# Attention and gated FFN layer on one core: mask copies on VectorE, the first group's maxima as rows without DRAM, one transpose per group, raw weights spread over four batches

## The reference, cut to what matters

```python
# x: (8, 512, 256); 16 heads of 16; Wq, Wk, Wv: (16, 256, 16); FFN 256 -> 768 -> 256
q, k, v = (einsum('btc,hcd->bhtd', x, W) + b  for (W, b) in (q, k, v))
scores  = einsum('bhtd,bhsd->bhts', q, k) * 0.25
probs   = softmax(scores + causal)                    # over s <= t
y       = einsum('bhts,bhsd->bhtd', probs, v).reshape(8, 512, 256)
x = layernorm(x + y @ Wo + bo)
wq8(w)  = w.astype(float8_e4m3fn).astype(float32)      # the FFN weights are rounded to FP8
fuse = silu((x @ wq8(gate_w)) * gate_s) * ((x @ wq8(up_w)) * up_s)
x = layernorm(x + (fuse @ wq8(down_w)) * down_s)
```

## Time and profile before

| | |
|---|---|
| median of 3 runs | 587.77 us (587.28 to 589.21) |
| the profiled execution, its own time | 586.83 us |
| its span | 585.1 us, 1.73 us less than its time |
| PE (matmul) busy | 541.7 us, 93% |
| PE weight loads | 358.9 us, 61% |
| VectorE (DVE) | 457.4 us, 78% |
| ScalarE (ACT) | 324.9 us, 56% |
| GpSimd (POOL) | 232.0 us, 40% |
| mean granted TensorE clock | 0.971 |
| DMA | 68.22 MB, mean 117 GB/s |

### The profile page before, as it was taken

The page is one execution under the profiler, slowest core; times in us unless marked ns, Lnnn a source line. Parts: engine busy times, 40 slices in busy tenths (PEclk is TensorE's granted clock), DMA queues, the critical chain, the costliest instruction groups (busy, mean ns, idle before and its releaser), DMA issues.

```text
span 585.1 us, 10840 instructions
## 1 busy us (share of the span) xinstructions
PE 541.7 (93%) x4002; PEld 358.9 (61%) x4002; DVE 457.4 (78%) x805; ACT 324.9 (56%) x579; POOL 232.0 (40%) x253
## 2 busy tenths in 40 slices
PE   8358799999999999999999999988899999999992
PEld 4134346556556565665655655645468888888892
DVE  6875657788888888888878888887546898888885
ACT  3005546766767667766676676764764444355440
POOL 8204332434333443353243433331245444565442
PEclk9698979999999999999999999999899999999997
DMA  6692847456454654553745654430000011110112
GB/s 217 179 269 84 256 112 201 146 148 186 149 141 157 190 153 150 135 185 112 201 146 148 177 160 140 144 78 3 2 1 0 2 37 36 37 38 0 38 37 72
DMA packets 59615, 68.22 MB, mean 117 GB/s; under 512 B 4074, under 2 KB 53866, under 8 KB 59562
## 3 DMA queue, kind: packets, MB, share of 16 engines
q1 hardware_dynamic: 58710, 66.59, 38.7%
q10 hardware_dynamic: 852, 0.93, 0.5%
HBM read 37.63 MB, written 29.62 MB: 115 GB/s over the span
## 4 chain that ended last, share of the span: by engine, by line
PE 82%; DVE 5%; DMA 5%; issue 3%; ACT 2%; POOL 1%; SPq 0%; POOLq 0%; DVEq 0%; ACTq 0%
PE ps L1068 15%; PE ps L939 13%; PE ps L931 12%; PE ps L856 9%; PE ps L848 9%; PE ps L1077 7%; PE ps L915 7%; PE ps L916 4%; PE ps L879 2%; DVE nmax L611 2%; PE ps L872 2%; DMA m_scratch<-mrow 2%; PE ps L890 1%; DVE part L561 1%; DMA q_st<-zero_rows 1%
## 5 line engine op out<-in xcount | busy, mean ns | idle before, releaser
L611 DVE TENSOR_REDUCE nmax<-ps 128x2 f32<-128x1024 f32 (+1 forms) x192 | 196.9, 1041 | 74.2 <-PE ps L916 73.9
L447 ACT ACTIVATE probs<-ps 128x512 f32<-128x512 f32 x320 | 183.4, 594 | 83.9 <-PE ps L931 83.7
L370 POOL TENSOR_SCALAR_AFFINE_SELECT probs<-probs 128x512 f32<-128x512 f32 x128 | 86.5, 689 | 204.6 <-ACT probs L447 204.6
L931 PE MATMUL ps<-q_st,k_st 98*128 98x384 bf16 (+3 forms) x512 | 123.3, 304 | 9.0 <-DMA q_st<-m_scratch 5.3
L915 PE MATMUL ps<-k_st,q_st 98*128 98x256 bf16 (+2 forms) x384 | 83.2, 277 | 15.6 <-DMA k_st<-k_scratch 9.3
L398 POOL TENSOR_TENSOR f_l<-f_full,f_h 128x512 fp32r<-128x512 f32 x48 | 63.4, 1323 | 73.0 <-ACT f_h L532 73.0
L916 PE MATMUL ps<-k_st,q_st 124*128 124x128 bf16 x512 | 85.0, 222 | 0.0
L939 PE MATMUL ps<-probs,v_st 128*32 128x512 f32 (+3 forms) x1024 | 84.8, 450 | 0.2
L931 PEld LDWEIGHTS ps<-q_st,k_st 98*128 98x128 bf16 x512 | 44.2, 98 | 54.7 <-issue 27.4
L527 ACT ACTIVATE sgate<-ps,s_gate 128x512 f32<-128x512 f32 x48 | 32.8, 685 | 60.0 <-PE ps L1068 60.0
L915 PEld LDWEIGHTS ps<-k_st,q_st 98*128 98x128 bf16 x384 | 37.8, 99 | 37.3 <-issue 18.6
(11 more groups left out here) (94 smaller groups left out, 852.2 us busy)
## 6 DMA issues: line engine op xcount, KB each, us to landing
q_st<-q_scratch SPq DMA_DIRECT2D x32, 384.0 KB
k_st<-k_scratch SPq DMA_DIRECT2D x32, 384.0 KB
q_scratch<-part SPq DMA_DIRECT2D x16, 384.0 KB, 3.6
k_scratch<-part SPq DMA_DIRECT2D x16, 384.0 KB, 2.6
xT<-in_attn_xT SPq DMA_DIRECT2D x8, 512.0 KB, 3.9
q_scratch<-part SPq DMA_DIRECT2D x16, 256.0 KB, 3.8
resid<-in_attn_x SPq DMA_DIRECT2D x8, 512.0 KB, 3.7
k_scratch<-part SPq DMA_DIRECT2D x15, 256.0 KB, 2.1
```

Source lines behind the costliest of these rows:

```text
L370: pool.affine_select(out=blocks, in_=blocks, compare_op=ALU.is_ge, fill=0.0, base=0, pattern=[*pattern, [1, P]], channel_multiplier=-1).th ...
L447: act.activation(probs[:, u, :], ps[:, u % 2, :], ACT.Exp, scale=SCALE).then_inc(exp_done, 1)
L611: dve.tensor_reduce(nmax[:, i, heads[0]:heads[-1] + 1], src, AX.X, ALU.max, negate=True).then_inc(max_taken, 1)
L931: m = pe.matmul(ps[:, u % 2, c0:c0 + T - P * j], k_st[0:RP, g, h, P * j:P * j + P], q_st[0:RP, g, h, P * j:T], start=True, stop=True)
```

## The change

- **Masks.** All four `fill_mask` copies run on VectorE: q for groups 0-1 and 2-3 at the start, k for groups 0-1 after the first two `first_lo`, k for groups 2-3 after the last two.
- **First maxima.** For w = 0, `first_rows` makes 16 transposes of 2 columns each, into PSUM banks 0 and 6, with the two parts on partitions 0 and 1; ScalarE and VectorE copy two heads each straight into q_st (2 x 1024). `scores(0, 0)` waits for these copies, and no DMA is left between them.
- **One transpose.** `transpose_max` is one transpose of all 32 columns of mpart; mrow becomes 32 partitions x 128, and `m_scratch` is laid out accordingly, so that rows of 256 B instead of 1 KB are stored, and 256 B pieces are read.
- **Order on TensorE.** `scores(0, 0)`, `scores(0, 1)` and the first half of the projection work stand among the maxima of group 1; fewer `keep_warm` there, 12 instead of 4 before the first stack.
- **DMA order.** b_o leaves the start (now with the late constants), xT of batch 1 goes behind the first two stacks, x of batch 0 and gate_w behind mrow of group 1; up_w is loaded in batch 1 and down_w in batch 3, behind the stacks of the next batch.
- **Quantizing.** No steps for w = 0 and 1; three for w = 2 to 29, six for w = 30 and 31.
- **add_bias** of batch n runs at g = 1 of batch n itself, the first too.

```diff
@@ -30,8 +30,8 @@
...
     HW = 32
-    NCONST = 3
-    NLATE = 4
+    NCONST = 2
+    NLATE = 5
@@ -42,7 +42,7 @@
...
     k_scratch = nc.dram_tensor("k_scratch", (H * D, NP, T), BF16, kind="Internal").ap()
-    m_scratch = nc.dram_tensor("m_scratch", (G, RM * HG, T), BF16, kind="Internal").ap()
+    m_scratch = nc.dram_tensor("m_scratch", (G, TB, RM, HG, P), BF16, kind="Internal").ap()
@@ -94,7 +94,7 @@
...
         mpart = carve(TB * 2 * HG, BF16).rearrange("p (b a h) -> p b a h", b=TB, a=2)
-        mrow = carve(T, BF16)
+        mrow = carve(P, BF16)
@@ -115,6 +115,8 @@
...
+        row_halves = [ps[0:RM, bank, :].bitcast(BF16) for bank in (0, YB)]
@@ -141,6 +143,7 @@
...
         mT_full, mT_out = sem("mT_full"), sem("mT_out")
+        rows_full, rows_out = sem("rows_full"), sem("rows_out")
@@ -206,7 +209,7 @@
...
                 eng.wait_ge(lo_ready[k], B)
-                eng.wait_ge(mrow_stored[k], 16 * B)
+                eng.wait_ge(mrow_stored[k], 16 * (B if k else B - 1))
@@ -241,11 +244,12 @@
...
                 sp.wait_ge(mT_out, n * G + g + 1)
-                sp.dma_start(m_scratch[g], mrow[0:RM * HG, :]).then_inc(mrow_stored[g], 16)
+                sp.dma_start(m_scratch[g].rearrange("i a h p -> (i a h) p"), mrow[0:TB * RM * HG, :]).then_inc(mrow_stored[g], 16)
...
             def load_mrow(n, g):
-                sp.wait_ge(mrow_stored[g], (n + 1) * 16)
-                sp.dma_start(q_st[0:RM, g], m_scratch[g].rearrange("(a h) t -> a h t", h=HG)).then_inc(mrow_loaded[g], 16)
+                sp.wait_ge(mrow_stored[g], (n + 1 if g else n) * 16)
+                sp.dma_start(q_st[0:RM, g].rearrange("a h (i p) -> a h i p", i=TB),
+                             m_scratch[g].rearrange("i a h p -> a h i p")).then_inc(mrow_loaded[g], 16)
@@ -267,21 +271,18 @@
...
             sp.dma_start(w_v[:], wv.rearrange("(k p) n -> p k n", p=P)).then_inc(const_in, 16)
-            for dst, src in ((b_v, bv), (b_o, bo)):
-                sp.dma_start(dst[:], src.partition_broadcast(P)).then_inc(const_in, 16)
-            load_xT(1)
+            sp.dma_start(b_v[:], bv.partition_broadcast(P)).then_inc(const_in, 16)
...
             sp.dma_start(k_scratch[0:P, 0:3, :], part[:, 1, :, :]).then_inc(part_stored[1], 16)
-            sp.wait_ge(mask_filled, 2)
+            sp.wait_ge(mask_filled, 3)
...
             load_stack(0, 1)
+            load_xT(1)
...
             store_parts(0, 3)
-            sp.wait_ge(mask_filled_late, 3)
+            sp.wait_ge(mask_filled, 4)
             load_stack(0, 2)
-            load_raw(0)
-            load_x(0)
@@ -289,22 +290,24 @@
...
                 if n == 0:
-                    load_raw(1)
                     sp.dma_start(w_o[:], wo.rearrange("(k p) n -> p k n", p=P)).then_inc(late_in, 16)
-                    sp.dma_start(s_down[:], down_s.partition_broadcast(P)).then_inc(late_in, 16)
+                    for dst, src in ((b_o, bo), (s_down, down_s)):
+                        sp.dma_start(dst[:], src.partition_broadcast(P)).then_inc(late_in, 16)
...
                         sp.dma_start(dst[:], src).then_inc(late_in, 16)
+                    load_x(0)
+                    load_raw(0)
...
                 load_mrow(n, 2)
-                if n == 0:
-                    load_raw(2)
...
                     load_stack(n + 1, 1)
+                if n in (1, 3):
+                    load_raw((n + 1) // 2)
@@ -349,14 +352,11 @@
...
             pool.memset(k_st[0:RM, 2:G].rearrange("p g h t -> p (g h t)").bitcast(F32), ONES).then_inc(mask_filled_late, 1)
-            pool.wait_ge(pool_const, CONSTS)
-            for stack, rows in ((q_st, mask_q), (k_st, mask_k)):
-                fill_mask(pool, stack, rows, 2).then_inc(mask_filled_late, 1)
...
                 if n == 0:
-                    pool.wait_ge(const_in, 16 * NCONST)
+                    pool.wait_ge(late_in, 16 * NLATE)
@@ -374,15 +374,14 @@
...
-            add_bias(0)
...
                         lo_part(n + 1, g)
-                    if g == 1 and n + 1 < B:
-                        add_bias(n + 1)
+                    if g == 1:
+                        add_bias(n)
@@ -428,9 +427,9 @@
...
                 act.wait_ge(mT_full, w + 1)
-                if w:
-                    act.wait_ge(mrow_stored[(w - 1) % G], ((w - 1) // G + 1) * 16)
-                act.activation(mrow[0:RM * HG, :], max_bf[0:RM * HG, 0:T], ACT.Copy).then_inc(mT_out, 1)
+                v = w - 1
+                wait(act, mrow_stored[v % G], (v // G + 1 if v % G else v // G) * 16)
+                act.activation(mrow[0:TB * RM * HG, :], max_bf[0:TB * RM * HG, 0:P], ACT.Copy).then_inc(mT_out, 1)
@@ -474,11 +473,9 @@
...
                 mid_part(0, m, probs[:, m, :])
-            empty_mT(0)
-            act.wait_ge(mT_out, 1)
-            act.dma_start(m_scratch[0], mrow[0:RM * HG, :]).then_inc(mrow_stored[0], 16)
-            act.wait_ge(mrow_stored[0], 16)
-            act.dma_start(q_st[0:RM, 0], m_scratch[0].rearrange("(a h) t -> a h t", h=HG)).then_inc(mrow_loaded[0], 16)
+            act.wait_ge(rows_full, 1)
+            act.activation(q_st[0:RM, 0, 0:2, :].rearrange("a h t -> a (h t)"), row_halves[0], ACT.Copy).then_inc(mT_out, 1)
@@ -549,7 +546,8 @@
...
             dve.wait_ge(pool_const, 5 + MG)
-            fill_mask(dve, q_st, mask_q, 0).then_inc(mask_filled, 1)
+            for g in (0, 2):
+                fill_mask(dve, q_st, mask_q, g).then_inc(mask_filled, 1)
@@ -596,6 +594,10 @@
...
+            def first_step(w):
+                return 3 * (w - 2) + 3 * max(w + 2 - W, 0)
@@ -675,9 +677,8 @@
...
                 first_lo(k + 1)
-                if k == 0:
-                    dve.wait_ge(pool_const, 6 + 2 * MG)
-                    fill_mask(dve, k_st, mask_k, 0).then_inc(mask_filled, 1)
+                dve.wait_ge(pool_const, 6 + 2 * MG)
+                fill_mask(dve, k_st, mask_k, k).then_inc(mask_filled, 1)
@@ -688,6 +689,9 @@
...
                     take_max(w, u)
+                    if w and u == 0:
+                        dve.wait_ge(mT_full, 1)
+                        dve.tensor_copy(q_st[0:RM, 0, 2:4, :].rearrange("a h t -> a (h t)"), row_halves[1]).then_inc(rows_out, 1)
@@ -696,7 +700,8 @@
...
                         take_max(w + 2, 0)
-                    quantize(3 * w)
+                    if w > 1:
+                        quantize(first_step(w))
@@ -719,7 +724,8 @@
...
                         normalize_y(w - 1)
-                    quantize(3 * w + 1)
+                    if w > 1:
+                        quantize(first_step(w) + 1)
@@ -730,11 +736,16 @@
...
                         empty_v(n + 1, 1)
-                    quantize(3 * w + 2)
+                    if w > 1:
+                        quantize(first_step(w) + 2)
...
                         split_max(w + 2)
+                    else:
+                        for q in range(3):
+                            quantize(first_step(w) + 3 + q)
@@ -868,9 +879,16 @@
...
                     pe.wait_ge(ynT_out, 2 * (w // G - 1) + w % G)
-                for i in range(TB):
-                    m = pe.transpose(max_bf[0:RM * HG, P * i:P * i + P], mpart[:, i].rearrange("p a h -> p (a h)"), ident_bf[:])
-                m.then_inc(mT_full, 1)
+                pe.transpose(max_bf[0:TB * RM * HG, 0:P], mpart.rearrange("p i a h -> p (i a h)"), ident_bf[:]).then_inc(mT_full, 1)
+            def first_rows():
+                pe.wait_ge(mpart_ready, 1)
+                for v in range(2):
+                    for h in range(2):
+                        for i in range(TB):
+                            m = pe.transpose(row_halves[v][:, T * h + P * i:T * h + P * i + P], mpart[:, i, :, 2 * v + h], ident_bf[:])
+                    m.then_inc(mT_full if v else rows_full, 1)
@@ -903,12 +921,13 @@
...
                     if w == 2:
-                        pe.wait_ge(mask_filled_late, 3)
+                        pe.wait_ge(mask_filled_late, 1)
+                        pe.wait_ge(mask_filled, 4)
...
                 wait(pe, max_taken, NM * w + u - 1)
-                if u == 1:
-                    wait(pe, mT_out, w)
+                if u == 1 and w > 1:
+                    pe.wait_ge(mT_out, w)
@@ -918,8 +937,11 @@
...
                 g = w % G
-                if u == 0:
-                    pe.wait_ge(mrow_loaded[g], (w // G + 1) * 16)
+                if w == 0 and u == 0:
+                    pe.wait_ge(mT_out, 1)
+                    pe.wait_ge(rows_out, 1)
+                elif u == 0:
+                    pe.wait_ge(mrow_loaded[g], (w // G + 1 if g else w // G) * 16)
@@ -978,22 +1000,16 @@
...
             last[0] = (0, "v", 1)
-            keep_warm(4)
+            keep_warm(12)
...
             pe.wait_ge(zeros_loaded, 16)
-            pe.wait_ge(mask_filled, 2)
+            pe.wait_ge(mask_filled, 3)
...
                     keep_warm(2)
-            scores_max(1, 0)
-            transpose_max(0)
-            for u in range(1, NM):
```

(24 more changed lines are left out.)

## The result

The changed kernel takes 571.58 us in the median of 4 runs (569.98 to 572.4), the kernel before 588.29 (587.28 to 589.21) on the same chip: a ratio of 0.972 (0.9699 to 0.9741). That is 16.7 us faster where 25 were forecast, and just above the range. The profiled execution took 571.63 us with a span of 569.9, which is 15.2 us less than the profiled execution before; what follows is counted between these two.

A forecast was written before the change was run, and what follows sets the result against it. It took TensorE as the bound (82% of the chain of waits), with DMA and VectorE waits in the first 86 us. Start -19.5, steady step -6.5, end +1.0 make -25.0: 561.8 from 586.83, stated as 562.8 for the median, range 558 to 571.

The forecast's parts named there:

- First stack: Start to first score: mask copies off POOL shorten first_lo; first score at 21.7 us instead of 26.17, a gain of 4.5.
- To scores(0, 0): First score to scores(0, 0): DRAM trip replaced by transposes and copies, 10.1 us instead of 18.4, reached at 31.8.
- to transpose_max(1): scores(0, 0) to transpose_max(1): VectorE's 5.4 us of group 1 maxima, no gain, reached at 37.2.
- (2): transpose_max(1) to transpose_max(2): fewer quantize steps and smaller transposes, 9.3 us instead of 10.1, reached at 46.5.
- To scores_max(4, 0): transpose_max(2) to scores_max(4, 0): its stack arrives behind mrow(2), reached at 58; stall 2.2 us instead of 4.36.
- the term for the queue: Loads ahead of mrow(2): 3.75 MB from 40.5 us at 335 GB/s, 11.2 us, done at 51.7.
- To scores(3, 0): scores_max(4, 0) to scores(3, 0): 9.0 us at full clock instead of 11.9, reached at 67.0; the start gains 19.5.
- The DMA queue keeps the start: Rival: start queue delivers 239, not 335 GB/s; stall grows 4.5 us, clock falls, total 570.0; chance 0.17.
- The steady step: Attention loop: one transpose instead of four saves 0.24 us a step, 27 times, 6.5 us; bounds 0 and 8.
- The two DMA terms of the step at nothing: Steady steps: 256 B mrow pieces, and up_w and down_w delaying one trip each by 2.4 us, hidden by 3.9 spare.
- VectorE sets the steady pace: Rival: VectorE, busy 83.60 of 100 us, paces the steady steps; one transpose saves nothing, total 569.3; chance 0.13.
- End of attention: Before the FFN: quantize steps not done early come last, TensorE waits 1.0 us (0.6 to 1.5).

The follow-up runs named there:

- consts_first: The changed kernel with b_o, s_down and the two scale vectors issued at the very start, behind b_v: 568.88 us, ratio 0.9676.
- x1_late: The changed kernel with only x of batch 1 moved from ahead of mrow of group 2 to behind the stacks of batch 1: 569.96 us, ratio 0.9695.
- four_transposes: The changed kernel with transpose_max, mrow and m_scratch as in the kernel before (four transposes, 1 KB rows): 574.8 us, ratio 0.9786.
- xraw_early: The changed kernel with x of batch 0 and gate_w issued ahead of mrow of group 1: 570.77 us, ratio 0.9722.
- mrow_act: The changed kernel with the store of mrow of group 2 alone issued by ScalarE's queue, its load still by SP: 570.76 us, ratio 0.9698.
- best2: The changed kernel with late constants and x(0) loaded at the start, x(1) behind batch 1's stacks, dummy matmuls in steps 0 and 30: 565.51 us, ratio 0.961.
- gap_warm: The changed kernel with ten dummy matmuls in step 30, where TensorE waits for the normalization: 568.48 us, ratio 0.9666.

## Why the prediction was wrong, step by step

- **First stack** (21.7, was 22.64). Right in kind: first_lo fell from 7.57 to 1.47 us for two. The k store took 4.15 in place of the 4 or so that I allowed, and the last first_lo ended at 12.9, not 12.05. That is the whole 0.9, and it lies within the spread: six other traces whose kernels are the same up to here have their first score at 21.64 to 22.74.
- **To scores(0, 0)** (10.1 us, was 10.2), **to transpose_max(1)** and **(2)** (5.4 and 9.3, were 5.4 and 9.3). Right. VectorE's copy of the rows took 0.67 where I had 1.2; the 16 transposes took 1.05.
- **To scores_max(4, 0): the step that failed.** It asked when the stack arrives behind mrow(2), and never when TensorE wants mrow(2) itself, at scores(2, 0). With the forecast 51.7 for the end of the queue that would have done little harm: store and load of 1.4 and 2.1 us, as at 38.82 and 57.57 above, put the rows in at some 55.2, 1 us behind TensorE by its pace here (an estimate). What failed under it is the term for the queue, 3.75 MB at 335 GB/s. The bytes were added wrongly: the transfers named make 3846 KB, which is 3.94 MB and 3.75 only in units of 1024 KB. And the old queue as a whole moved 291 GB/s, with one constant copied to 128 partitions in it, where the new one holds two. The 3.94 MB took from 40.8 to 57, 246 GB/s, 16.2 us for the 11.2 forecast. At the rate of 48 to 55 us, 382 GB/s, the 0.77 MB of 43 to 48 us would have taken 2.0 us and not 5: the slow phase is by this estimate 3 us of the 5.9 by which mrow(2) was late; consts_first gives 1.8 back. That the store was issued at 51.94, and not at 48.2 when the copy was ready, cost little by itself: in x1_late it was issued at 47.37, and the rows came 1.2 us earlier, about what 0.52 MB less ahead of them are worth.
- **To scores(3, 0)**, forecast with the full clock. The wait of 4.54 us took the clock to 0.50 from 58.4 to 65 us. In the kernel before the same happened behind 70 us: the 0.77 of the earlier trace rows is the start of it, and 0.50 stands until 80. So stall and slow clock did not go, they moved one stage up. Two of the prediction's own signs of being wrong came with them: a wait on an m_scratch load inside the loop, from the backlog and not from the small pieces, and scores(3, 0) later than 72. Start: 12.7 gained for 19.5, **6.8 of the error of 9.8**.
- **The rival "The DMA queue keeps the start"**, 570.0 with a chance of 0.17, named cause and size: 239 GB/s (246 measured), 4.5 us more stall, and the clock. It missed the place, which is a stage earlier, and that its total of 570.0 comes near 571.58 is in part luck: it holds 6.5 us for the steady step, which gave 3.8. I gave it too little: its evidence, a DMA share above 0.95 in both windows, was there, while the 335 GB/s left the slow start of its queue out.
- **The steady step** (0.24 us saved, was 0.146 from transpose_max(4) to (28), 281.78 for 285.28). The mechanism was right, the term mis-sized: I took 0.32 for four to be 0.08 each, and one alone holds the chain for 0.16. From 0.16 and 0.32 a further transpose costs 0.053. That agrees with the 56 ns that the Trainium skill (TensorE: Matmul & The Clock Gate, "Back-to-back issue gap") gives for the isolated gap at 128 columns: the estimate of 4.5 us by the page was the better one, and I went by the mean of a row that holds a fixed part. **2.7 of the error** by transpose_max(30). four_transposes confirms it by itself.
- **The two DMA terms of the step at nothing.** Right for TensorE: no wait on m_scratch shows after scores(2, 0). But the 256 B pieces are not free. They make the trip 0.7 us longer (four_transposes), which the 3.9 us to spare hide.
- **The rival "VectorE sets the steady pace"** is refuted: TensorE is busy 99.33 of 100 us as before, with VectorE at 85.02.
- **End of attention** (1.0 lost). TensorE waits 0.36 us for the last quantize. But step 30, which I did not cost at all, loses 0.9: TensorE's idle time there was 3.22 us in the kernel before and is 3.42 now, and this trace comes out of it at half clock, where before the clock fell only 1.5 us later, at 411.3. From transpose_max(31) to the FFN 19.0 us for 18.8. Together 1.2 lost, by another way than the one named, so that the total is right by luck. It need not be the change that does it: in xraw_early and mrow_act the clock falls late, as in the kernel before, and 0.5 is lost.

The parts alone, from the runs that undo them: masks 3.2 us, first rows without DRAM 4.2 (7.9 in the one execution traced), one transpose 3.2. The raw weights over four batches, the new order of quantizing and that of add_bias were not undone by themselves. The weights are what makes room ahead of mrow(2) for x and the constants, and xraw_early shows how little room there is.

**Open.** What in the constants slows the queue: each is read by 128 partitions from the same KB, and the start of consts_first shows that w_o is not needed for it, but no run changes how they are read. What stretches SP's issues. And why the clock was down behind 3.42 us of idle time in some traces and fell only 1.5 us later in others, with the same idle time, or why it stayed up to the FFN in best2 and not in gap_warm, with the same ten matmuls. So the 3.1 us of gap_warm have no shown cause.

## What to carry to other kernels

When loads are moved earlier in a shared queue, write down for every small transfer behind them the bytes ahead of it and the instant at which its reader wants it; price the bytes at the slowest rate seen for their kind, not at the best. A pair or four of one instruction in a row tells the slope and the fixed part only together with a row of one. And a wait of a few microseconds on TensorE costs the clock behind it too: behind the 4.54 us of wait, the half clock cost 2.1 more up to scores_max(4, 0). An effect of 1 us on one stretch is to be looked for in several traces, as here two without the edit show what one with it does.

## What the runs showed of the hardware that was not expected

- Two constants copied to 128 partitions hold a full queue at 63 to 148 GB/s for 3 us, where it moves 382 just after; at the start of consts_first, with hardly anything else queued, 64 GB/s.
- SP's own issue instructions grow from 0.43 us to 1.4, and to 2.03 in mrow_act, in the stretch in which the DMA engines are behind. The backlog alone does not do it: with the engines as busy at 60 us (333 GB/s) the issues took 0.32 to 0.65, and the longest in the kernel before, 2.17 us at 81.59, met engines that had had only 8 KB to move since 78 us.
- 8 KB on a second, empty queue needed 6.4 us beside that backlog.
- 8 KB stored and read back in 256 B pieces took 0.7 us longer than in 1 KB pieces (2.25 for 1.54 us on average), and the issue of the load 0.62 us for 0.24.
- VectorE copied two rows of 1024 BF16 elements from PSUM in 0.67 us, about the time of 512 on ScalarE in the earlier trace rows.
